# The weighting of the chosen experts moves from GpSimd to VectorE in a mixture-of-experts layer

## The reference

```python
def _L1_ffn_ref(hidden_states, gate_w, e_bias, gate_proj, up_proj, down_proj, shared_gate_w, shared_up_w, shared_down_w):
    HIDDEN, INTER, N_EXPERTS, N_GROUP, TOPK_GROUP, TOP_K, SCALING = 128, 64, 16, 4, 2, 4, 2.5
    ...
    topk_idx, topk_weight = _gate(x, gate_w, e_bias)
    g = jnp.einsum('th,eih->eti', x, gate_proj)
    u = jnp.einsum('th,eih->eti', x, up_proj)
    inter = jax.nn.silu(g) * u
    expert_out = jnp.einsum('eti,ehi->eth', inter, down_proj)
    sel = expert_out[topk_idx, jnp.arange(T)[:, None]]
    y = jnp.einsum('tkh,tk->th', sel, topk_weight)
    ...
    shared_out = jax.nn.silu(sg) * su @ shared_down_w.T
    return y + shared_out
```

## Time and profile before

| | |
|---|---|
| median of 3 runs | 1727.69 us (1726.05 to 1727.95) |
| the profiled execution's own time | 1729.74 us |
| its span, first to last instruction | 1728.0 us |
| mean granted TensorE clock | 0.944 of full |
| PE busy | 1539.1 us (89%) |
| DVE busy | 1394.3 us (81%) |
| ACT busy | 922.2 us (53%) |
| POOL busy | 395.9 us (23%) |
| the two calls of `experts_top4` | some 122 us (from 1380.5) and 116 us (from 1609.6) of the span |

### The profile page before, as it was taken

One profiled execution on the slowest core, in us unless ns is written; L12 is line 12 of the kernel. 1 busy time (PEld: TensorE's weight loads), 2 busy tenths in 40 slices (PEclk: granted clock), 3 DMA queues, 4 the chain that ended last, 5 costly groups with the idle time before them and its releaser, 6 DMA issues. The chain is left out here.

```text
span 1728.0 us, 24116 instructions
## 1 busy us (share of the span) xinstructions
PE 1539.1 (89%) x8528; PEld 771.3 (45%) x8528; DVE 1394.3 (81%) x2384; ACT 922.2 (53%) x1748; POOL 395.9 (23%) x430
## 2 busy tenths in 40 slices
PE   6899999999999999699997898868999689876798
PEld 2111111111111111288873333326888577566687
DVE  6999999999999993576656999997666578489774
ACT  3188888888888888442236566553322332211322
POOL 3200000000000000000016878870000234332234
PEclk7599999999999999899999999999999879998799
DMA  3341100000000001000002222210000022100122
GB/s 104 118 127 30 33 26 23 23 23 23 23 23 23 31 18 43 15 1 1 1 1 68 69 68 65 70 55 1 1 1 1 1 67 83 50 1 1 50 87 87
DMA packets 41232, 66.35 MB, mean 38 GB/s; under 512 B 11422, under 2 KB 18383, under 8 KB 40392
## 3 DMA queue, kind: packets, MB, share of 16 engines
q1 hardware_dynamic: 41112, 64.82, 12.2%
HBM read 57.02 MB, written 6.88 MB: 37 GB/s over the span
## 5 line engine op out<-in xcount | busy, mean ns | idle before, releaser
L884 DVE TENSOR_REDUCE row_max<-ps 128x1 f32<-128x1024 f32 x512 | 600.9, 1219 | 33.7 <-PE ps L689 17.5
L807 ACT ACTIVATE probs<-ps 128x512 f32<-128x512 f32 x1024 | 528.9, 604 | 126.9 <-PE ps L704 126.6
L704 PE MATMUL ps<-q_stack,k_stack 51*128 51x512 bf16 x1024 | 346.2, 386 | 8.7 <-ACT probs L807 6.7
L689 PE MATMUL ps<-k_stack,q_stack 48*128 48x512 bf16 x1024 | 325.1, 403 | 20.3 <-DVE row_max L884 10.6
L721 PE MATMUL ps<-probs,v_head 128*16 128x512 f32 x2048 | 269.8, 599 | 0.0
L689 PEld LDWEIGHTS ps<-k_stack,q_stack 48*128 48x128 bf16 x1024 | 58.4, 96 | 368.0 <-DVE row_max L884 342.0
L1397 PE MATMUL ps<-s_hc,ident 128*128 128x512 f32 x256 | 139.0, 628 | 47.8 <-DVE s_hc L1670 42.7
L1050 ACT ACTIVATE x_gate<-ps 128x512 f32<-128x512 f32 x128 | 76.3, 598 | 184.7 <-PE ps L221 184.6
L1322 POOL TENSOR_TENSOR s_dbx<-s_dx,s_b_rows 128x512 f32<-128x512 f32 x128 | 159.4, 1269 | 35.1 <-DVE s_h L1661 34.5
L1661 DVE TENSOR_TENSOR_SCAN s_h<-ps,s_state,s_dbx 128x512 f32<-128x512 f32 x128 | 156.5, 1261 | 4.6 <-POOL s_dbx L1322 2.8
L704 PEld LDWEIGHTS ps<-q_stack,k_stack 51*128 51x128 bf16 x1024 | 76.0, 93 | 131.8 <-ACT probs L807 128.2
(11 more groups left out here) (343 smaller groups left out, 2037.1 us busy)
## 6 DMA issues: line engine op xcount, KB each, us to landing
s_b_rows<-s_b_dram SPq DMA_DIRECT2D x64, 256.0 KB, 3.1
y_spread<-y_probs_dram SPq DMA_DIRECT2D x128, 128.0 KB, 3.0
q_stack<-q_parts_dram SPq DMA_DIRECT2D x30, 96.0 KB
k_stack<-k_parts_dram SPq DMA_DIRECT2D x30, 96.0 KB
w_w<-w_dram SPq DMA_DIRECT2D x1, 2048.0 KB, 7.9
o_dram<-o_sb SPq DMA_DIRECT2D x64, 32.0 KB
q_stack<-q_parts_dram SPq DMA_DIRECT2D x30, 64.0 KB
k_stack<-k_parts_dram SPq DMA_DIRECT2D x30, 64.0 KB
```

The source lines that it names most:

```text
L689: last = nc.tensor.matmul(core.ps[:, 2 * b + r, :], qst[buf][0:KROWS, u * P:(u + 1) * P], kst[buf][0:KROWS, key:key + CH], start=True, sto ...
L704: nc.tensor.matmul(core.ps[:, S_BANK + n % S_RING, :], kst[buf][HALF:ROWS, kt * P:(kt + 1) * P], qst[buf][HALF:ROWS, c * CH:(c + 1) * CH], ...
L807: nc.scalar.activation(probs[:, us % RING, c * CH:(c + 1) * CH], core.ps[:, S_BANK + n % S_RING, :], ACT.Exp).then_inc(exp_done, 1)
L884: nc.vector.tensor_reduce(mx[:, u, b:b + 1], core.ps[:, 2 * b:2 * b + 2, :], mybir.AxisListType.XY, ALU.max).then_inc(max_done, 1)
```

## The change

GpSimd's multiplication of `gate` by `spread` is taken out of its queue, 8 in each chunk, 32 in each call, 64 in all. The same multiplication stands in VectorE's `multiply(g)`, directly ahead of the product with the up half. The waits for ScalarE's `gate_done` and for the transfer (`spread_loaded`) go with it. The semaphore `scaled` is raised by VectorE now, and VectorE waits for it itself; SyncE's wait for `scaled` (before it loads into a ring tile again) stands as it was. GpSimd keeps the layer norms' roots.

```diff
             ln.root(pool, 1)
             for g in range(LAST):
                 c, u = g // UNITS, g % UNITS
-                if u:
-                    m = c * PAIRS + u - 1
-                    pool.wait_ge(gate_done, g + 1)
-                    pool.wait_ge(spread_loaded[m % P_RING], 32 * (m // P_RING + 1))
-                    nc.gpsimd.tensor_tensor(gate[g % SETS][:], gate[g % SETS][:], spread[m % P_RING][:],
-                                            ALU.mult).then_inc(scaled, 1)
                 if u == 7 and c + 2 < NC_:
                     ln.root(pool, c + 2)
...
             def multiply(g):
                 c, u = g // UNITS, g % UNITS
                 rows = slice(0, rows_of(u))
+                dve.wait_ge(gate_done, g + 1)
                 if u:
-                    dve.wait_ge(scaled, c * PAIRS + u)
-                else:
-                    dve.wait_ge(gate_done, g + 1)
+                    m = c * PAIRS + u - 1
+                    dve.wait_ge(spread_loaded[m % P_RING], 32 * (m // P_RING + 1))
+                    nc.vector.tensor_tensor(gate[g % SETS][:], gate[g % SETS][:], spread[m % P_RING][:],
+                                            ALU.mult).then_inc(scaled, 1)
+                    dve.wait_ge(scaled, m + 1)
                 dve.wait_ge(up_done, 2 * g + 2)
                 if g >= SETS:
                     dve.wait_ge(down_done, g - SETS + 1)
```

## The result

| | before | after |
|---|---|---|
| median of the runs (lowest to highest) | 1727.82 us (1726.05 to 1728.47), 4 runs | 1712.55 us (1708.09 to 1715.76), 4 runs |
| the profiled execution's own time, span | 1729.74, 1728.0 us | 1715.76, 1714.0 us |

The changed kernel is 15.3 us faster: ratio 0.9905, 95% interval 0.9885 to 0.9925. 1709 was predicted, in a range of 1703 to 1718. The profiled execution of the changed kernel is the slowest of its four runs; 2.8 us of its time lie in the layers ahead of the first call (chunk 0 of y1 starts at 1395.0 us before and at 1397.8 after), where nothing was changed. The eleven other traces of this document have that start between 1392.2 and 1396.5. So the stages have to be compared with each other, not the spans.

A forecast was written before the change was run, and what follows sets the result against it. TensorE was taken to set the pace, losing some to a late `hidden`. Gains of 12.6 (chunks 1 and 2), 5.3 (chunk 3 of y1) and 1.1 (chunk 3 of y2) sum to 19.0 us: 1727.7 becomes 1709, range 1703 to 1718.

The forecast's parts named there:

- chunk 2, y1: Second chunk after chunk 0 in call y1: falls from 24.9 to 21.7 us, a gain of 3.2.
- chunk 3, y1: Last chunk of call y1: shorter chain of product, statistics and root, first pair and last unit, together 5.3 us gained.
- chunk 1, y2: Call y2: falls from 27.3 to 23.2 us, a gain of 4.1, part of it TensorE's clock.
- chunk 2, y2: Call y2: falls from 25.3 to 21.7 us, a gain of 3.6.
- The price of the multiplication: On VectorE, 64 times: 0.68 us each, the pair with the product 1.34 us instead of 0.61.
- uneven side work: VectorE, units 1 to 5: needs 10.9 us against TensorE's 9.1, costing 0 to 1.8 us a chunk, taken as 0.5.
- The stand-still: Small VectorE instructions starting during GpSimd's multiplication wait until it ends; its removal gives 12.6 us in chunks 1 and 2.
- the case that the root comes first every time: Seven or eight GpSimd roots each hold up a new multiplication by 1.01 us: the gain is 15 instead of 19.0.
- Rival 2: Multiplication costs 1.3 us on VectorE as on GpSimd: slower, 1732; turning point 1.1 us; chance 0.06.
- Rival 1: VectorE becomes the bound, a pair costing 1.55 instead of 1.34: half the gain, 1714 to 1718; chance 0.13.
- Rival 3: Waits only move to the transfer, TensorE's gaps being its own: under 4 us gained, 1724 to 1727.7; chance 0.04.
- Rival 4: VectorE never holds TensorE up and all clock drops vanish, chunk 0's too: 1703 or less; chance 0.03.

The follow-up runs named there:

- y1_only: Against the kernel before, the multiplication moved to VectorE in call y1 alone, y2 left on GpSimd: 1718.10 us, ratio 0.9946.
- y2_only: Against the kernel before, the multiplication moved to VectorE in call y2 alone, y1 left on GpSimd: 1721.95 us, ratio 0.9972.
- root_later: Kernel before, GpSimd still multiplying, with the three roots for the following norm one unit later in its queue: 1720.67 us, ratio 0.9947.
- early_probs: Changed kernel with the next chunk's expert weights turned after unit 6, not 7, and copied at unit 8, not the next unit 0: 1707.00 us.
- idle_gpsimd: Changed kernel with GpSimd still multiplying constant tiles at the same places, its result read by nobody: 1743.27 us, ratio 1.0093.
- extra_half: Changed kernel with a further VectorE multiplication of 128x256 on idle tiles in each of the 64 pairs: 1718.82 us, ratio 0.994.
- again: The changed kernel measured and traced a second time, with nothing altered: 1712.28 us, ratio 0.9909.

## Why the prediction was right, and where its terms were off

The direction and the mechanism held: the small instructions no longer stand still, the chain in chunk 3 is shorter, and VectorE carries the multiplication nearly for nothing. What each term of the sum was worth is read from four traces with each form of each call: y1_only and y2_only give a sample of both forms, and root_later gives one of the form before. In chunk 3 of y1 root_later differs, and there are three. "Before" and "after" are means of the chunk's length in us:

| term | predicted | before | after | measured |
|---|---|---|---|---|
| chunk 1, y1 | 1.7 | 24.96 | 23.61 | 1.4 |
| chunk 2, y1 | 3.2 | 24.18 | 22.04 | 2.1 |
| chunk 3, y1 | 5.3 | 28.23 | 22.30 | 5.9 |
| chunk 1, y2 | 4.1 | 25.90 | 23.39 | 2.5 |
| chunk 2, y2 | 3.6 | 24.98 | 23.27 | 1.7 |
| chunk 3, y2 | 1.1 | 19.06 | 17.76 | 1.3 |
| sum | 19.0 | | | 14.9 |

The sum of 14.9 agrees with the 15.3 us between the medians (14.9 and 13.6 when both kernels were measured again). It is 4.1 below the sum predicted. The number came as near as it did partly by luck: chunk 3 of both calls gave 0.8 more than said, which hides part of the 4.9 that chunks 1 and 2 fell short.

*The step that was mis-sized* is "27.3 - 23.2 = 4.1 (y2)" and "25.3 - 21.7 = 3.6": 7.7 predicted, 4.2 measured. Two things are in it. The lengths before were those of one execution. It had the gap of 2.61 us and the clock of 0.94 and 0.93 in it, and three other traces of the same code have chunk 1 in 24.97, 26.22 and 25.16 us. The prediction even priced this part ("some 1.6 us"), but took it as always there. And chunk 2 after the change was set at 21.7 with the transfer hidden. It comes to 22.4 to 23.65, since in three of four traces the store of the weights took 2.9 to 3.3 us instead of 1.6, and VectorE waited for it. early_probs takes that away and has the 21.8. In y1's chunk 2 the prediction took 24.9 for before; the four traces have 24.85, 24.79, 23.56 and 23.51. Most of the rest of the 4.1 us is there (3.2 predicted, 2.1 measured).

*The price of the multiplication* was right: 0.691 us for 0.68, the pair 1.33 for 1.34. VectorE fitted: chunk 1 was 23.3 to 24.0 against 23.2, chunk 2 of y1 22.0 against 21.7. So 0.5 us a chunk for uneven side work was somewhat low.

*The stand-still* goes with the change as said, and idle_gpsimd, which brings it back, loses 31 us. Two readings beside it went too far. "Small VectorE instructions that start during line 1969 stand still until it is over" doesn't hold for all of them. In the trace before, y2's chunk 2, three multiplications run in a row from 1685.48 to 1689.27:

```profile
1685.48 3.79 POOL L1969 TENSOR_TENSOR y_gate<-y_gate,y_spread 128x512 f32<-128x512 f32 x3 [2.26 <-DMA y_spread<-y_probs_dram]
1686.90 1.22 DVE L2164 TENSOR_TENSOR y_g_beats<-y_g_beats,y_g_ties 128x64 f32<-128x64 f32 x1
1688.15 0.22 DVE L2165 TENSOR_REDUCE y_g_rank<-y_g_beats 128x16 f32<-128x64 f32 x1
1688.41 0.90 DVE L2167 TENSOR_SCALAR y_g_rank<-y_g_rank 128x16 f32<-128x16 f32 x1
```

The reduction in their midst (line 2165) takes its usual 0.22 us, and the instructions before and behind it stand still. All 28 slow ones of that trace are TENSOR_TENSOR (18) or TENSOR_SCALAR (10). And the clock was said to be 1.00 in both chunks of y1 "that had no such long gap". Chunk 2 of y1 had one of 2.09 us, with the clock at 1.00:

```profile
1456.58 1.16 PE L2018 MATMUL ps<-w_w_down,y_hidden 128*128 128x128 f32 x8 [2.09 <-DVE y_hidden L2116]
```

So one gap of 2 us doesn't always come with a lower clock, and how much of y2's gain is the clock isn't shown.

*Chunk 3 of y1*: 4.02 us a unit for 4.2. The wait for the root is 0.18, not 0.4; the statistics and the normalisation were as reckoned. The root started 0.16 behind the multiplication and was longer by 0.38 us, as if it had begun its work 0.54 behind the multiplication's start. That agrees in direction with the Trainium skill's rule ("SBUF — State Buffer", "Who interferes with whom"), by which the one that starts second waits for the first. In the direction that speaks against the change, a root holding up a multiplication, nothing is seen: the longest of the 64 is 0.694. The prediction gave a gain of 15 us for the case that the root comes first every time, without working it out; the gain came to 15, but the root never came first, so this agreement is chance.

*Chunk 0*: at nothing, as said; 29.5 in both calls of the trace before and of all three traces of the changed kernel. In y2 it took 28.7 once with each form (root_later before, y2_only after), at a clock of 0.94 for 0.88. TensorE's clock stayed at 1.00 in chunks 1 and 2, and its waits came to 3.9 us, just under the 4 to 7.

*The rivals.* Rival 2's turning point of 1.1 us is borne out by the line through the two kernels with extra work; the changed kernel is 0.4 us from it. Rival 1 gave 1714 to 1718 for a pair of 1.55; extra_half, with 1.54, came to 1718.8. Rival 3 (waits only move to the transfer) holds for a part: it took back some 1.5 us in y2's chunk 2, and with y1's chunk 3 early_probs recovers 4 to 5. Rival 4's chunk 0 didn't move, and its clock stayed 0.88.

*Still open*: why the kernel before was some 2 us slower on root_later's chip; and what made the store slow. Over the slow store (trace after, 1663.8 to 1667.1) the queues' rows show an instruction load of 0.02 MB beside it, and so they do in the two other slow cases. Over the quick one of again only the first of these rows stands; over some other quick ones such a load stands behind the store's packets. It was seen together, and not tried apart. Nor does a run separate the two ways in which the change brings `hidden` forward in chunks 1 and 2: small instructions no longer stand still, and the path itself is shorter (0.73 us on VectorE in place of 1.27 us on GpSimd and the hand-over).

```profile
q1 hardware_dynamic: 32, 0.03, 3.8%
q8 instruction: 1, 0.02, 2.1%
```

## What to carry to other kernels

When GpSimd and VectorE both work from SBUF, add up what GpSimd's instruction costs the other engine's small ones before counting it as free: here 64 rows of 1.27 us cost 31 us of the program though nobody waited for them (beside a VectorE that was already nearly full), while the same work on VectorE was 0.73 us each and mostly hidden. When an engine takes over work, look which of the old owner's waits come with it (here the transfer), and move what feeds them ahead: that was worth another 4 to 5 us. If the old owner's queue holds other engines' work, try its order first: root_later had two thirds of one chunk's gain without moving anything to VectorE. And take the lengths before from more than one execution: a stage with long gaps and a lower clock in one trace had neither in the next.

## What was not expected of the hardware

The same call of the same program took 97.1 to 101.4 us (y2 of the kernel before) in four traces. The longest of them has gaps of 2.61 and 2.09 us ahead of `hidden` and a clock of 0.94 and 0.93 in those two chunks; the shortest has no gap over 0.89 there and a clock of 1.00 in chunks 1 to 3. It doesn't follow that each gap lowers the clock: y1_only has one of 2.10 us in chunk 1 of y2, with 1.00. A VectorE reduction ran at its usual 0.22 us while TENSOR_TENSOR and TENSOR_SCALAR on either side of it stood still for GpSimd. And a store of 0.03 MB to DRAM, 1.6 us from its issue to the loads behind it, took 2.9 to 3.3 us in three of the four traces with y2 changed, at the same place of the program. In the two traces of the kernel before, none of the 16 stores took over 1.8.
